# A graph layer's neighbour product moved ahead of the gather, beside the edge counting

## What is computed

```
xn    = (x - mean) / sqrt(var + eps)            # per row
own   = xn @ wc                                 # 512 x 512
near  = segment_sum((xn @ wn)[src], dst) / degree
x     = x + own + near + bias                   # then causal attention, experts, second layer
```

## Time and profile before

| | us |
|---|---|
| three runs | 1540.17, 1543.76, 1544.21 (median 1543.76) |
| the profiled execution | 1544.43 |
| its span, first to last instruction | 1542.4 |
| PE busy in the span | 1431.5 (93%) |
| DVE / ACT / POOL busy | 1005.8 / 722.6 / 610.9 |
| start of the stage `graph_causal` on PE | 137.83 |
| start of the query products | 216.42 |
| mean granted clock of PE | 0.983 of full |

### The profile page before, as it was taken

One profiled execution on the slowest core, in us unless ns is written; L12 is line 12 of the kernel. 1 busy time (PEld: TensorE's weight loads), 2 busy tenths in 40 slices (PEclk: granted clock), 3 DMA queues, 4 the chain that ended last, 5 costly groups with the idle time before them and its releaser, 6 DMA issues. The chain is left out here.

```text
span 1542.4 us, 22146 instructions
## 1 busy us (share of the span) xinstructions
PE 1431.5 (93%) x8094; PEld 892.3 (58%) x8094; DVE 1005.8 (65%) x1848; ACT 722.6 (47%) x1410; POOL 610.9 (40%) x507
## 2 busy tenths in 40 slices
PE   4888999999988899999999899889989999988998
PEld 3554555547777744444556545446676776866664
DVE  7998244325666603343354514678999999999995
ACT  5452114335666511110111320347788887787784
POOL 4788200041455200000000070018786785776863
PEclk9999999999999999999999999999999999999999
DMA  7002000043433050000000400012120110101001
GB/s 253 1 1 86 1 0 1 0 106 109 78 65 66 18 218 0 1 1 0 0 0 1 168 0 0 1 39 58 28 43 1 36 22 14 36 5 31 1 1 67
DMA packets 38185, 60.12 MB, mean 39 GB/s; under 512 B 17206, under 2 KB 21946, under 8 KB 37694
## 3 DMA queue, kind: packets, MB, share of 16 engines
q1 hardware_dynamic: 36766, 56.13, 13.5%
q10 hardware_dynamic: 1312, 2.56, 0.5%
HBM read 33.15 MB, written 5.87 MB: 25 GB/s over the span
## 5 line engine op out<-in xcount | busy, mean ns | idle before, releaser
L1524 POOL TENSOR_TENSOR tl_ex<-tl_ex,tl_left 128x1250 f32<-128x1250 f32 x79 | 207.3, 2624 | 32.8 <-ACT tl_left L1859 28.4
L1334 DVE SCALAR_TENSOR_TENSOR X<-ex_ps_x,g,X 128x512 f32<-128x512 f32 x80 | 59.7, 750 | 163.2 <-PE ex_ps_x L1233 163.2
L1666 PE MATMUL tl_banks<-identf,tl_ex 128*128 128x128 f32 x800 | 133.9, 282 | 20.1 <-ACT tl_pt L1880 10.8
L1880 ACT COPY tl_pt<-tl_banks 128x512 f32<-128x512 f32 (+1 forms) x200 | 108.2, 541 | 94.3 <-PE tl_banks L1666 93.7
L2034 POOL TENSOR_TENSOR lo<-xn,hi 128x512 f16<-128x512 f32 x5 | 5.9, 1189 | 349.8 <-ACT hi L2140 349.8
L1233 PE MATMUL ex_ps_x<-w,hid 128*128 128x512 f32 (+1 forms) x320 | 141.1, 592 | 0.0
L1221 PE MATMUL ex_ps_h<-yt,w 128*128 128x512 f32 (+1 forms) x384 | 140.0, 518 | 0.0
L1666 PEld LDWEIGHTS tl_banks<-identf,tl_ex 128*128 128x128 f32 x800 | 88.8, 141 | 85.8 <-issue 48.8
L1282 ACT ACTIVATE hid<-ex_ps_h,b 128x512 f32<-128x512 f32 (+1 forms) x48 | 29.1, 608 | 222.5 <-PE ex_ps_h L1221 222.4
L1950 DVE MAX8 tl_m<-tl_banks 128x8 f32<-128x1250 f32 x80 | 116.3, 1454 | 10.0 <-PE tl_banks L1634 9.9
L1956 DVE MAX8 tl_m<-tl_left 128x8 f32<-128x1250 f32 x80 | 117.1, 1464 | 2.7
(11 more groups left out here) (282 smaller groups left out, 2980.3 us busy)
## 6 DMA issues: line engine op xcount, KB each, us to landing
tl_kl<-tl_KT SPq DMA_DIRECT2D x16, 320.0 KB, 4.3
tl_qs<-tl_QO SPq DMA_DIRECT2D x16, 320.0 KB, 5.7
kl<-KT SPq DMA_DIRECT2D x14, 320.0 KB, 4.4
qs<-QO SPq DMA_DIRECT2D x14, 320.0 KB, 5.9
w<-in_L_ffn_W SPq DMA_DIRECT2D x8, 512.0 KB, 8.3
w<-in_L_ffn_W SPq DMA_DIRECT2D x4, 1024.0 KB, 9.0
at_kept<-AT SPq DMA_DIRECT2D x1, 3200.0 KB, 9.0
AT<-at_kept SPq DMA_DIRECT2D x1, 3200.0 KB, 10.8
```

The costliest lines, as they stand in the source:

```text
L1524: pool.tensor_tensor(ex[:, n % EXS, 0:N], ex[:, n % EXS, 0:N], left[:, n % LEFT, :], ALU.subtract).then_inc(s_probs, 1)
L1666: mm = pe.transpose(ps_t[:, b * P:(b + 1) * P], ex[:, n % EXS, a + b * P:a + (b + 1) * P], m.identf[:, :])
L1880: act.copy(pt[:, n % PTS, a:a + w], ps_t[:, 0:w]).then_inc(s_kept, 1)
```

## The change

The product with `wn` is taken before the gather. In the counting stage each node tile gets four more products, `far = xn @ wn` (new `far_rows`), ACT copies the sum twice (float32 `far` and float16 `hi`), POOL makes `lo = far - hi`. In `graph_causal` the gather then gives `near` itself: the count matrix is the stationary operand, `hi` and `lo` (512 columns) are the moving ones, 200 matmuls; `agg`, its copies and the ten `near` products are gone. The statistics are taken in two halves of five node tiles. The steps beside the counting start at edge tile 36 instead of 66 and come every 27 tiles instead of 24.

```diff
-    rows_at = {66 + 24 * t: t for t in range(NT)}
-    cols_at = {70 + 24 * t: t for t in range(NT)}
-    own_at = {75 + 24 * t + 5 * k: (t, k) for t in range(NT) for k in range(KD)}
+    rows_at = {36 + 27 * t: t for t in range(NT)}
+    cols_at = {40 + 27 * t: t for t in range(NT)}
+    own_at = {43 + 27 * t + 3 * k: (t, k) for t in range(NT) for k in range(KD)}
+    far_at = {55 + 27 * t + 3 * k: (t, k) for t in range(NT) for k in range(KD)}
+    low_at = {55 + 27 * t + 3 * KD + 9: t for t in range(NT)}
+    mean_at = {10: range(0, 5), **{50 + 4 * t: [t] for t in range(5, NT)}}
+    var_at = {10: range(0, 5), **{60 + 6 * t: [t] for t in range(5, NT)}}
+    centre_at, dev_at = {10: 0, 88: 1}, {10: 0, 118: 1}
+    invert_at, shift_at = {36: 0, 130: 1}, {38: 0, 132: 1}
...
             sp.dma_start(wc[:, :, :], rows_of(io["L0_gnn_wc"])).then_inc(s_wc, 16)
+            sp.dma_start(wn[:, :, :], rows_of(io["L0_gnn_wn"])).then_inc(s_wn, 16)
...
             def low(t):
-                pool.wait_ge(s_high, t + 1)
-                pool.tensor_tensor(lo[:, t, :], xn[:, t % XR, :], hi[:, t, :], ALU.subtract).then_inc(s_low, 1)
+                pool.wait_ge(s_side_kept, side["far", t] + 1)
+                pool.tensor_tensor(lo[:, t, :], far[t % YR][:, :], hi[:, t, :], ALU.subtract).then_inc(s_low, 1)
...
+            def far_rows(t, k):
+                bank = ps_s[:, side["far", t] % 2, :]
+                if k == 0:
+                    open_side("far", t)
+                    if t == 0:
+                        pe.wait_ge(s_wn, 16)
+                mm = pe.matmul(bank[:, :], xt[:, t % XT, k, :], wn[:, k, :], start=(k == 0), stop=(k == KD - 1))
+                if k == KD - 1:
+                    mm.then_inc(s_side, 1)
...
+            def keep_far(t):
+                v = side["far", t]
+                act.wait_ge(s_side, v + 1)
+                if t >= YR:
+                    act.wait_ge(s_low, t - YR + 1)
+                act.copy(far[t % YR][:, :], ps_s[:, v % 2, :])
+                act.copy(hi[:, t, :], ps_s[:, v % 2, :]).then_inc(s_side_kept, 1)
```

In `graph_causal` (the scratch `ht` moves to where `agg` was, so that SP's first fetch of head 1 now waits for the seventh value product):

```diff
+                if h == 1:
+                    sp.wait_ge(s_v_ps, NT - VLAG + 2)
...
+            def gather(t):
+                if t >= 3:
+                    pe.wait_ge(s_added, t - 2)
+                for a in range(NT):
+                    if a == NT - 1:
+                        pe.wait_ge(s_flip_kept, 1)
+                    for part in (hi, lo):
+                        mm = pe.matmul(ps_n(t), m.A[:, a, t * P:(t + 1) * P], part[:, a, :],
+                                       start=(a == 0 and part is hi), stop=(a == NT - 1 and part is lo))
                 mm.then_inc(s_near, 1)
...
-            gather(0)
-            gather(1)
+            for t in range(0, 7):
+                gather(t)
+            turn_x(0)
+            for t in range(7, NT):
+                gather(t)
             pe.wait_ge(s_weights, weights_done)
-            for t in range(0, 4):
-                near(t)
-            gather(2)
-            turn_x(0)
-            for t in range(4, NT):
-                near(t)
...
-            for a in range(NT):
-                dve.tensor_reduce(m.deg_s[:, a:a + 1], m.AT[:, a, :], AX_X, ALU.add).then_inc(s_sums, 1)
...
+            degrees(0, 3)
+            add(0)
+            degrees(3, 6)
+            add(1)
+            add(2)
+            degrees(6, NT)
+            add(3)
             scales(0)
```

More of the change, by code:

```diff
@@ L92, in window, with graph_in @@
     return min(max((t * SLOPE >> 6) - REACH, 0), N - WIN)
-def graph_in(nc, m, io, space, wc, own, hi, lo, ahead):
+def graph_in(nc, m, io, space, wc, wn, own, hi, lo, ahead):
     NC = -(-N // CD)
     CW = CD * NT
-    XR, XT = 3, 2
+    XR, XT, YR = 2, 2, 2
+    HALVES = (range(0, NT // 2), range(NT // 2, NT))
     def spans(t):
@@ L118, in graph_in @@
         flips_at.setdefault(min(closes[c] + LATER, ET - 1), []).extend((c, j) for j in whole(c))
-    rows_at = {66 + 24 * t: t for t in range(NT)}
-    cols_at = {70 + 24 * t: t for t in range(NT)}
-    own_at = {75 + 24 * t + 5 * k: (t, k) for t in range(NT) for k in range(KD)}
+    rows_at = {36 + 27 * t: t for t in range(NT)}
[7 more added lines that the diff above has]
+    invert_at, shift_at = {36: 0, 130: 1}, {38: 0, 132: 1}
     side = {}
[L124 to L127, removed]
+    for t in range(NT):
+        for kind in ("cols", "own", "far"):
+            side[kind, t] = len(side)
     by_pool = [t for t in range(HOTS, ET) if t % HOTS and t % 5 in (1, 3)]
@@ L230, in _ @@
                     half_hot(t)
[L231 to L234, removed]
+                if t in shift_at:
+                    shifts(shift_at[t])
+                if t in low_at:
+                    low(low_at[t])
         @block.vector
@@ L299, in _ @@
                 dve.wait_ge(s_cols, 2)
-                for chunks in (range(0, 3), range(3, NC)):
-                    if chunks[0]:
-                        invert()
+                for i, chunks in enumerate((range(0, 3), range(3, 11), range(11, NC))):
+                    if i:
+                        invert(i - 1)
                     with dve.Fori(chunks[0], chunks[-1] + 1) as c:
@@ L471, in keep_cols @@
                 if t >= XT:
-                    act.wait_ge(s_side, side["own", t - XT] + 1)
+                    act.wait_ge(s_side, side["far", t - XT] + 1)
                 act.copy(xt[:, t % XT, :, :], ps_s[:, v % 2, :].rearrange("p (k c) -> p k c", k=KD)
@@ L486, in _ @@
             for t in range(ET):
[L487 to L493, removed]
+                if t in mean_at:
+                    means(mean_at[t])
+                if t in centre_at:
+                    centre(centre_at[t])
+                if t in var_at:
+                    variances(var_at[t])
+                if t in dev_at:
+                    deviation(dev_at[t])
                 if t in rows_at:
@@ L499, in _ @@
                     keep_own(own_at[t][0])
+                if t in far_at and far_at[t][1] == KD - 1:
+                    keep_far(far_at[t][0])
                 for c in range(NC):
@@ L512, with graph_causal @@
 VLAG = 5
-def graph_causal(nc, m, io, space, hi, lo, own, wn, s_weights, weights_done, spill, recips, wqkv, gains, QO, KT, V, ahead):
+def graph_causal(nc, m, io, space, hi, lo, own, s_weights, weights_done, spill, recips, wqkv, gains, QO, KT, V, ahead):
     TN = H * NT
-    CUTS = pieces(NP)
     bands = scale_groups()
+    DEGREES = [(0, 3), (3, 6), (6, NT)]
     HTS = VLAG + 2
@@ L975, in _, with degrees @@
         def _(dve):
[L976 to L980, removed]
+            def degrees(a, b):
+                for t in range(a, b):
+                    dve.tensor_reduce(m.deg_s[:, t:t + 1], m.AT[:, t, :], AX_X, ALU.add).then_inc(s_sums, 1)
+                done = b + 2 * DEGREES.index((a, b))
+                dve.wait_ge(s_sums, done)
+                dve.tensor_tensor(deg[:, a:b], m.deg_s[:, a:b], m.padded[:, a:b], ALU.add).then_inc(s_sums, 1)
+                dve.wait_ge(s_sums, done + 1)
+                dve.reciprocal(deg[:, a:b], deg[:, a:b]).then_inc(s_sums, 1)
+                dve.wait_ge(s_sums, done + 2)
             def add(t):
@@ L1051, in _ @@
                               None, ALU.mult).then_inc(s_gained, 1)
-            keep_sum(2)
+            for t in range(4, 7):
+                add(t)
             scale_cols(0)
-            for t in range(4, 8):
-                add(t)
+            add(7)
             scales(1)
```

95 lines of the change are left out of this document (39 added, 56 removed).

## The result

| | before | changed |
|---|---|---|
| median of five runs, us | 1540.17 (1538.39 to 1544.21) | 1530.42 (1529.40 to 1532.72) |
| the profiled execution / its span | 1544.43 / 1542.4 | 1529.86 / 1528.1 |
| start of `graph_causal` on PE (the flip) | 137.83 | 158.74 |
| start of the query products | 216.42 | 202.90 |
| first scores of head 1 | 362.05 | 345.21 |

The ratio is 0.9931, 95% interval 0.9912 to 0.995: faster, by 9.75 us of the medians, where 11.8 was forecast. Three points of PE tell the story: the flip comes 20.9 us later, the way from there to the query products is 34.4 us shorter, so the query products start 13.5 us earlier.

A forecast was written before the change was run, and what follows sets the result against it. POOL was taken to pace the old counting and PE `graph_causal`, with PE bounding the new counting. Flip 22.6 us later less 34.4 back gives -11.8, 1532.6, forecast 1532 us; range 1519 to 1543.

The forecast's parts named there:

- 34.4 us back in `graph_causal`: First gather to query product: 78.04 us falls to 43.7, the ten `near` products gone, no new wait.
- the bound of 1.4 us: Early `graph_causal`: DVE's new scales held by POOL could make PE stand 0 to 1.4 us; 0 taken.
- 12.7 us per node tile: Counting stage: 11.5 us PE work, 0.85 standing for `xt`, 0.33 average for other ACT copies in the way.
- PE becomes the bound, POOL does not: Counting stage: POOL set the old pace; now PE bounds at 0.43 us per edge tile, POOL needing 10.6 per 27.
- First transposes at 28.7, tail of 1.3 us: Counting stage: side work's first transposes at 28.7; 1.3 us from last counting matmul to the flip.
- Flip at 160.4: Start of `graph_causal`: 159.1 plus 1.3 for the clock, 22.6 us later than 137.83.
- The clock: Before edge tile 40: half the chance of one clock fall that doubles 2.7 us of work, 1.3 us.
- The fetch of head 1: SP's fetch waits some 3 us longer, for a value product; 20 us of cover, 3 us lost at most.
- PE's work alone counts: Rival, counting stage: ACT never in the way, node tile costs 11.5, 11.7 us less, 1520; chance 0.15.
- The hand-offs cost twice as much: Rival, counting stage: another 0.85 us per node tile gives +8.4, 1541; chance 0.18.
- The clock stays low: Rival, counting stage: repeated stands at `xt` make PE fall to 1.2 GHz, 1549 to 1555; chance 0.07.
- The counting hides all of it: Rival, counting stage: it stays at 137.8 and the whole 34.4 us come back, 1509; chance 0.05.

The follow-up runs named there:

- the roomy kernel: Changed kernel with next tile's transposes early, far products two edge tiles later, flips six edge tiles behind their chunk, last `lo` at the last edge tile: 1522.80, again 1521.93 us.
- control two: The changed kernel repeated unaltered beside later follow-up runs: 1528.61 us, ratio 0.991 to the kernel before.
- the statistics in halves alone: Kernel before with statistics in two halves and side work from edge tile 36 every 27, no far product, old gather: 1540.05 us, ratio 0.9992.
- Control one: The changed kernel repeated unaltered beside the first follow-up runs: 1528.36 us, ratio 0.9911 to the kernel before.
- the late start: Changed kernel with statistics in one go and side work from edge tile 66 every 25 tiles, without the wider hand-off spacing: 1549.17 us, ratio 1.0039.
- turning early: Changed kernel with the next node tile's transposes moved ahead of the last far product: 1527.83 us, ratio 0.9906 to the kernel before.
- two other kernels: Changed kernel without three of four partial `wc` products, 1504.95 us; changed kernel with POOL's `hot_b` share halved, 1527.00 us.

## Why the prediction was right, point by point

The forecast was 1532 us, and 1530.42 was measured. The mechanism came as told: PE alone in `graph_causal`, PE as the new bound of the counting, one hand-off per node tile. That the numbers lie so close is in part luck. The forecast started from 1543.76, the median of three runs; the five have 1540.17, and 11.8 less is 1528.4. And the lead at the query products is 13.5 us (20.9 - 34.4), not 11.8, since the node tiles were priced too high; the medians of the first comparison show 9.75, those beside the controls 13.1 and 14.4.

- **34.4 us back in `graph_causal`:** flip to query product took 78.59 before and 44.16 after, 34.43. No gap entered the gather. The hold of DVE by POOL was real, 1.03, 1.12 and 0.76 us on small operations, and the scales came 3.4 us before the transposes that need them; the 0 taken there stands, and the bound of 1.4 us was not used up. By the Trainium skill (SBUF — State Buffer, section Who interferes with whom) a VectorE instruction with two SBUF inputs contends with a GpSimd instruction that reads SBUF, and the later of the two blocks; the trace agrees, with ends within 0.02 us of POOL's. One of the two rows that the prediction names for this rule is not a case of it: `hot_m` (1.17 us under `lo`) compares one tile with a number per partition, so it has one tile as input, not two. That it is held too is measured; no run here asks why.
- **12.7 us per node tile:** 12.37 at full clock, in the profiled execution and in both controls alike. Bare work is 11.72 (the roomy kernel), 0.2 more than the 11.5 summed; the hand-offs add 0.65, not 0.85 + 0.33 (by the terms given for it, 1.40 + 0.3 - 0.77, the 0.85 is rather 0.93). The waits at `xt` were there, 6.3 us in seven of ten node tiles, but the 0.33 for collisions, worked out from the schedule alone, was too much: where a chunk copy stood ahead of `xt` (80.21 in ACT's timeline), PE stood 0.62 at the flip that wanted that copy, and then not for `xt`.
- **PE becomes the bound, POOL does not:** POOL waits 12.9 us for PE from 60 to 130, and half its work gone changes nothing. POOL's pace was at most 10.07 us per node tile, not 10.6. What the prediction says of the kernel before, that POOL sets its pace, is not shown: from 60 to 130 us PE waited longer for DVE's `hot_m` than for POOL's `hot_b`, and no run changed either engine's load there. The two were close, and the forecast used only the measured pace.

```profile
PE gi_ps_c L416 <- DVE hot_m L286: 3.8, 11, 0.6
PE gi_ps_c L416 <- POOL hot_b L216: 1.3, 2, 1.1
```

- **First transposes at 28.7, tail of 1.3 us:** 28.31; the tail took 1.30 (157.44 to 158.74) with one wait of 0.82 for the last `hot_b`.
- **Flip at 160.4:** 158.74. The start is 0.4 us early, eight steady node tiles are 2.6 us shorter; the first one, 14.67 against 12.7 + 1.3, takes 0.7 back, and the way from the last transposes to the flip, 16.8 against 16.1, another 0.7.
- **The clock:** half a chance of a fall worth 2.7 us, so 1.3 in the sum. The profiled execution had it, at 0.88 from 30 to 48, and others of the same kernel had not: 156.40 against 158.74, so a whole fall costs 2.3 to 2.8 us. The first node tile says the same: 14.67 us against 12.19 in control two at full clock. Half of that is 1.2: the size was right, and the chance was a guess that the executions seen neither bear out nor refute. The prediction tied the old fall to a wait of 2.67 us for ACT. That wait is gone, and the clock fell all the same, between 27 and 28 us, where PE was 60 to 70% busy in the two microseconds before and the longest wait near it is 0.61 us. Control two did the same work with the same waits and kept the full clock.
- **The fetch of head 1** cost nothing that can be seen: 142.3 us from the query products to the first scores of head 1. The kernel with the statistics in halves alone has the old fetch, and took 142.3 as well. In the profiled execution of the kernel before it was 145.6, and there the clock fell, as the busy time by stretch shows for before (first row) and for the changed kernel (second):

```profile
350.00:355.00 5.00, 5.00 (x42) 4.46 (x42) 1.61 (x3) 0.22 (x1) 0.00 (x0) 0.54 1.09 349
```

```profile
335.00:340.00 5.00, 5.00 (x50) 3.29 (x48) 2.07 (x5) 1.73 (x4) 2.77 (x2) 1.00 1.08 354
```

Control one, the changed kernel, had the fall as well (146.4 us for the same way), so it belongs to the execution, not to the change. It is one part of why the profiled executions lie 14.6 us apart and the medians 9.75: their lead is 13.5 us at the query products, 16.8 at the first scores of head 1 and 14.3 at the end of the span. The rest, the same code, took 1180.4 us before and 1182.9 changed, and 1184.7 and 1181.9 in the two controls. So single executions of one kernel differ by several microseconds (1526.20 to 1534.64 in control one), and a difference of 9.75 in medians of five is rough.

Of the rivals, *PE's work alone counts* is what the roomy order reaches: 1521.9 to 1522.8 where 1520 was given. *The hand-offs cost twice as much* did not come here; the late start shows that it needs only one copy in the wrong place: its node tiles take 13.58 us (57.15 to 165.81 in eight steps), where that rival had 12.7 + 0.85 = 13.55. *The clock stays low* is out for the change, 1.00 from 60 to 130 us in spite of the stands at `xt`; in the late start, with longer stands, it fell twice, for some 4 us each, and rose again. *The counting hides all of it* is out, with a flip 20.9 us later.

Open: why the clock fell in some executions near 28 and 335 us and not in others, with the same work. No run was made for it.

## What to carry to other kernels

When work moves under a stage with three nearly full engines, add up PE's own columns and the one longest chain through another engine per round: that sum gave the stage within 3% (12.7 against 12.37). Then lay the round out so that each copy has a few tiles of slack in *every* engine's order at once; taking away only the largest wait (turning early) let the next two take its place and gave 2.5 us at the flip, and all of them together gave 6. A split that lets the side work start sooner (halves of the statistics) pays where the engine that it fills is the bound: nothing that the time shows in the old kernel (3.06 us at the flip, 1.36 at the query products), 9 us in the roomy one.

## What was not expected of the hardware

- The clock can fall exactly at a hand-over between two stages, where the next one is all matmuls: 1.7 of 3.06 us won were given back there (flip at 134.77, matmuls 0.43 us apart until 138.94), and the same 1.7 in two other kernels.
- POOL's `hot_b` is not one duration: 0.60 to 0.80 us for the same 128x128 shape, and without its gap of 0.17 us when it follows a `lo`.
